# A causal attention and gated MLP kernel: who makes two of the sums of softmax weights, and when the third unit's x is loaded and rounded

## The reference, cut to what matters

```python
Q = _split_heads(x, H)                       # H = 16 heads of 16, B = 8, S = 1024, D = 256
K = _split_heads(x @ Wk + bk, H)
V = _split_heads(x @ Wv + bv, H)             # 1024 wide: 64 per head
scores = jnp.einsum('bhqd,bhkd->bhqk', Q, K) + mask       # causal, not scaled
attn = jax.nn.softmax(scores, axis=-1)
o = jnp.einsum('bhqk,bhkd->bhqd', attn, V)
...
a = x + jax.nn.gelu(o, approximate=False) @ Wf + bf
x = _layernorm(x + a)
...
x = _layernorm(x + (silu(x @ wg.T) * (x @ wu.T)) @ wd.T)   # int weights / 127
```

## Time and profile before

| | |
|---|---|
| time, median of 3 runs | 1847.62 us (1847.26 to 1853.65) |
| the profiled execution's own time | 1849.75 us |
| its span, first to last instruction | 1848.0 us |
| PE busy | 1762.1 us, 95% of the span |
| DVE busy | 1396.5 us, 76% |
| POOL busy | 1221.8 us, 66% (in stage B's slices 0.8 to 0.9, 0.1 to 0.2 in stage C) |
| ACT busy | 1050.4 us, 57% |

### The profile page before, as it was taken

How to read it: one execution, slowest core, us unless ns; L and a number is a source line. 1 busy time by engine, 2 the same in 40 slices (tenths; PEclk the granted TensorE clock), 3 DMA queues, 4 the chain that set the end, 5 groups by cost and what they waited for, 6 DMA issues and landing times. The chain is left out here.

```text
span 1848.0 us, 37611 instructions
## 1 busy us (share of the span) xinstructions
PE 1762.1 (95%) x10304; PEld 961.4 (52%) x10304; DVE 1396.5 (76%) x3417; ACT 1050.4 (57%) x1375; POOL 1221.8 (66%) x1146
## 2 busy tenths in 40 slices
PE   7999999999999999999999999888889999999996
PEld 5444444444444444444444444333466767676763
DVE  4787877778787787777778787886467878787864
ACT  2465665665565565665666565555545555555552
POOL 3488888888888888888888888999512222222221
PEclk9999999999999999999999999999999999999998
DMA  9675657556565655646556565563477565756500
GB/s 323 160 232 160 181 141 203 161 161 188 142 176 170 168 160 159 195 139 185 169 148 196 145 174 143 144 183 99 138 201 175 172 170 172 169 172 170 171 24 23
DMA packets 261152, 303.16 MB, mean 164 GB/s; under 512 B 28240, under 2 KB 177872, under 8 KB 261072
## 3 DMA queue, kind: packets, MB, share of 16 engines
q1 hardware_dynamic: 261072, 302.19, 58.3%
HBM read 174.20 MB, written 127.93 MB: 163 GB/s over the span
## 5 line engine op out<-in xcount | busy, mean ns | idle before, releaser
L802 POOL TENSOR_TENSOR weight_sum<-weight_sum,weights 128x512 f32<-128x512 f32 (+1 forms) x444 | 731.9, 1649 | 151.9 <-DVE weight_sum L1347 115.3
L1161 ACT ACTIVATE weights<-ring 128x1024 f32<-128x1024 f32 x576 | 570.7, 1026 | 221.2 <-PE ring L846 217.8
L846 PE MATMUL o_acc<-weights,v_pair 128*64 128x512 f32 (+3 forms) x3072 | 586.3, 501 | 17.1 <-POOL weights L757 16.4
L837 POOL TENSOR_TENSOR h_lo<-hidden,h_hi 128x512 f16<-128x512 f32 x96 | 114.4, 1193 | 390.2 <-ACT h_hi L1099 390.2
L1312 DVE TENSOR_REDUCE part_max<-ring 128x2 f32<-128x1024 f32 x256 | 301.0, 1217 | 86.4 <-PE ring L846 86.4
L846 PEld LDWEIGHTS o_acc<-weights,v_pair 128*64 128x64 f32 x3072 | 188.3, 136 | 302.7 <-issue 257.0
L1321 DVE CUSTOM_DVE_ANT_0 scrap<-ring,causal,part_max 128x256 bf16<-128x256 f32 (+3 forms) x512 | 251.3, 547 | 70.7 <-PE ring L846 70.4
L1321 DVE CUSTOM_DVE_ANT_0 scrap<-ring,causal 128x128 bf16<-128x128 f32 (+3 forms) x512 | 225.1, 486 | 91.1 <-PE ring L846 90.6
L846 PE MATMUL ring<-q_stack,k_stack 50*128 50x512 f32 (+3 forms) x1536 | 264.3, 382 | 26.1 <-DVE part_max L1312 17.6
L846 PE MATMUL ring<-k_stack,q_stack 48*128 48x512 f32 (+3 forms) x1536 | 256.9, 373 | 0.1
L846 PE MATMUL ring<-wf_sb,g 128*128 128x256 f32 x1024 | 230.5, 380 | 2.6 <-DVE y_pre L1416 1.7
(11 more groups left out here) (125 smaller groups left out, 2070.1 us busy)
## 6 DMA issues: line engine op xcount, KB each, us to landing
v_pairs<-v_unit SPq DMA_DIRECT2D x64, 512.0 KB, 3.5
v_pair<-v_pairs SPq DMA_DIRECT2D x64, 512.0 KB, 5.1
o_heads<-o_pair SPq DMA_DIRECT2D x64, 512.0 KB, 3.2
g<-o_heads SPq DMA_DIRECT2D x16, 2048.0 KB, 8.1
den_wide<-reciprocals SPq DMA_DIRECT2D x32, 1024.0 KB, 13.3
q_stack<-q_rows SPq DMA_DIRECT2D x128, 192.0 KB, 3.7
k_stack<-k_rows SPq DMA_DIRECT2D x128, 192.0 KB, 4.4
q_rows<-x_hi SPq DMA_DIRECT2D x28, 512.0 KB, 3.6
```

What stands on the lines that cost most here:

```text
L802: pool.tensor_tensor(dst, other, weights(t), ALU.add).then_inc(s_add, 1)
L837: pool.tensor_tensor(h_lo[:, f], h32[f % 2][:], h_hi[:, f], ALU.subtract).then_inc(s_hl, 1)
L846: return nc.tensor.matmul(o, l, r, start=start, stop=stop)
L1161: nc.scalar.activation(W[i][:], bank_of("t", i)[:], ACT.Exp).then_inc(s_w, 1)
```

## The change

Four things change. First, `begin_sum` moves from DVE (end of burst 2) to POOL, after the add of group 1. Second, POOL no longer adds group 8 (the ninth group, tile W7); DVE does, as the last sum of all (`last_sum`), at the head of burst 1 of the next step, after it has waited for all of POOL's adds of that pair. A new semaphore `s_add8` tells of it, and PE's `denominators` and ACT's exponential of W7 wait for it. Third, POOL's add of group 11 moves from the next step to the end of its own, and the masks of W7 and W8 now stand side by side. Fourth, the third unit's x: `load_x` comes right after the first stack loads on SP, ahead of five groups of stores, and `x_high` comes in burst 0 of step 0 on ACT.

```diff
-        ADDS = (1, 2, 3, 10, 7, 8, 9, 11)
+        ADDS = (1, 2, 3, 10, 7, 9, 11)
...
             load_stacks(0, 0)
+            load_x(ALONE, True)
             store_early_v(0, 0)
             store_early_k(0, 1)
             store_early_v(0, 1)
             store_early_k(1, 1)
             store_early_v(0, 2)
-            load_x(ALONE, True)
...
+            def begin_sum(rt, n):
+
+                pool.wait_ge(s_w, NU * n + use_of(5) + 1)
+                if rt >= 2:
+
+                    pool.wait_ge(s_den, n - 1)
+                    settle(pool, s_passed["pool"])
+                pool.tensor_tensor(acc1[rt % 2][:], weights(4), weights(5), ALU.add).then_inc(s_add1, 1)
...
                     mask(0, *m)
                     mask(1, *m)
-                if LEAD < r <= PAIRS + LEAD:
-                    add(11, r - LEAD - 1, n - LEAD - 1)
-                if now:
                     mask(2, *m)
                     if r < PAIRS:
-                        for t in (1, 2, 3):
-                            add(t, *m)
+                        add(1, *m)
+                    begin_sum(*m)
                 if r % 4 == 0 and unit_beside(r, it) is not None:
                     x_low(unit_beside(r, it))
                 if now:
+                    if r < PAIRS:
+                        add(2, *m)
+                        add(3, *m)
                     add(10, *m)
                     add(7, *m)
                     mask(7, *m)
-                    add(8, *m)
                     mask(8, *m)
                     add(9, *m)
+                    add(11, *m)
...
                 pe.wait_ge(s_add, NA * (n + 1))
+                pe.wait_ge(s_add8, n + 1)
...
+                    elif i == use_of(8):
+                        act.wait_ge(s_add8, n)
...
-                    if b == 3 and r % 4 == 0 and unit_beside(r, it) is not None:
+                    if b == (3 if r else 0) and r % 4 == 0 and unit_beside(r, it) is not None:
                         x_high(unit_beside(r, it), r == 0)
...
+            def last_sum(rt, n):
+
+                dve.wait_ge(s_add, NA * (n + 1))
+                dst = acc1[rt % 2][:, :, BANK - width_of(8):BANK]
+                v.tensor_tensor(dst, dst, weights(8), ALU.add).then_inc(s_add8, 1)
...
+                    if b == 1 and LEAD < r <= PAIRS + LEAD:
+                        last_sum(r - LEAD - 1, n - LEAD - 1)
...
-                    if b == 2 and LEAD <= r < PAIRS + LEAD:
-                        begin_sum(r - LEAD, n - LEAD)
```

More of the change, by code:

```diff
@@ L292, in build @@
         s_add = sem("sums_made")
+        s_add8 = sem("last_sum_made")
         s_den = sem("den_ready")
@@ L1334, in shift_turn @@
                             shift_parts[:].rearrange("p h m u -> p (h m u)").bitcast(F32)).then_inc(s_shs, 1)
-            def begin_sum(rt, n):
-                dve.wait_ge(s_w, NU * n + use_of(5) + 1)
-                if rt >= 2:
-                    dve.wait_ge(s_den, n - 1)
-                v.tensor_tensor(acc1[rt % 2][:], weights(4), weights(5), ALU.add).then_inc(s_add1, 1)
             def carry_sum(rt, n):
```

## The result

| | before | after |
|---|---|---|
| median of the runs | 1848.62 us (1847.26 to 1853.65, 4 runs) | 1830.3 us (1827.79 to 1832.5, 4 runs) |
| profiled execution, its span | 1848.0 us | 1830.8 us |
| ratio | | 0.9892, 95% interval 0.9876 to 0.9909 |

The changed kernel is 18.3 us faster (1.1%). (The kernel before has four runs here; the median that the forecast started from was that of three, 1847.62.)

The account below looks back on a forecast made before the run. PE was taken to bound the steps with projections, POOL the eight without. Terms -5.0 + 1 + 2 + 1 = -1 us on the median 1847.6 gave 1846.6 us, range 1833 to 1860.

Parts of the forecast that it names:

- Part one: Step 0, third unit's x loaded earlier: PE's 4.34 us wait and slow clock go, -5.0 us, bounds -5.8 and -3.
- The 1.2 us for the clock: Step 0, 42 to 50 us: six matmuls at reduced clock after PE's standstill lose 1.2 us or more, which goes too.
- The second pair's stacks: Step 0: PE wants these stacks 5.5 us earlier while their load time stays; 0.5 us taken off the gain.
- Part two, what goes: Steps with projections: PE's waits at T7 for DVE's maximum of S5 vanish, -1.35 us for four steps.
- Part two, what comes: Four steps with projections: new waits, 1.1 us in k = 0 and 1, 0.25 in k = 3, 0.1 at last_sum.
- The lock: DVE with two SBUF inputs and POOL reading SBUF exclude each other for a whole instruction; two meetings a step, before and after.
- Part three: Eight steps without projections: POOL stays the bound, 0.25 us a step charged for carry_sum queueing, +2 us, bounds -1 and +6.
- Part four: Steps 64 to 66: POOL takes over a sum, but last_sum holds up the first mask; +1 us, bounds -3 and +4.
- A: Rival, the sums are free: new waits covered, PE's 15.6 us come back, 1829 us; chance 0.21.
- Half of A: Half of what rival A expects from the sums coming free: 1837 us.
- B: Rival: DVE waits at last_sum in every step, T3 and T4 slip 0.4 us or more, 1870 us; chance 0.16.
- C: Rival: the early load of x gives nothing, colliding with the stacks or stalling V jobs, 1851.6 us; chance 0.09.

Follow-up runs that it names:

- e1: Kernel before with only the third unit's x loaded and rounded early, sums as they were: 1843.8 us, ratio 0.9964.
- e3: Kernel before without the first sum of the long half (W4 left out of the denominators), a measurement only: 1816.7 us, ratio 0.9828.
- e11: Changed kernel plus a spare addition on DVE of W7 + W7, ahead of the wait of last_sum: 1904.4 us, ratio 1.0302 to the kernel before.
- e7: Changed kernel with the last sum left out (W7 missing in the denominators), a measurement only: 1818.1 us, ratio 0.9828 to the kernel before.
- e12: Changed kernel plus a spare copy of W7 on DVE, ahead of the wait of last_sum: 1860.9 us, ratio 1.0055 to the kernel before.
- e2: Changed kernel with the third unit's x loaded and rounded where it was before, only the sums changed: 1838.4 us, ratio 0.9932 to the kernel before.
- e5: Changed kernel with, in steps k = 0, the next unit's x rounded in burst 1 and split ahead of begin_sum: 1821.2 us, ratio 0.9842 to before.
- e4: Kernel before with begin_sum still on DVE but at the head of burst 4, right ahead of carry_sum: 1854.6 us, ratio 1.0025.
- e6: Kernel e5 with DVE's carry_sum behind the maxima of S6 instead of ahead of them: 1856.1 us, ratio 1.0036 to the kernel before.
- e9: Kernel e5 with begin_sum back on DVE in the steps without projections (56 to 63): 1815.5 us, ratio 0.9815 to the kernel before.

## Why the prediction was wrong, point by point

**Part one, -5.0 us (bounds -5.8 to -3): right.** Measured -6.7 (4.1 to 9.4) by the runs, -3.8 and -5.9 in two traces. x was there at 29.45 us (I had said 29.8) and its split ended at 33.07 (33.3); PE's job came at 37.38 without a wait. The 1.2 us for the clock were not seen in after (the earlier trace rows has 0.79, and so has after) and were in e1. The second pair's stacks cost 0.61 us of named wait in after and 1.89 in e1, where I took 0.5.

**Part two, what goes: the step that failed.** "... the 46 waits make 0.34 us a step: -1.35 us for four steps." The mechanism was right: the waits went. The size was not: they were worth 2.4 to 2.7 us (pitch, e3). I took the named idle time for the price. (15.6 us over 46 waits is 0.34 a wait, not a step; the four waits that follow each other have 1.34 together.) Thirteen times 1.0 to 1.35 us is 13 to 18 us, more than the whole miss of this part, 10.5.

**Part two, what comes: +1.45 said, 1.86 measured.** 0.91 for the split of x and 0.46 at T4 make 1.37 against my 1.1; T8 in k = 3 cost 0.49 against 0.25; k = 1 and 3 cost nothing at `last_sum`. Short waits were again priced by their names.

**The lock: right**, in this kernel and in e11, e3 and e7, and wider than I had put it: e12 shows it for a copy, with one input. That it holds was also why handing a sum to GpSimd frees nothing by itself; the gain is that DVE has no sum ahead of S4 and S5.

**Part three, +2 (bounds -1 to +6): 1.1 lost in the trace,** but hardly for my reason. At full clock POOL is the bound, as I had said, and W4 comes 0.32 us late for it where I had charged 0.25. But less of its list is held up (17.09 us against 17.41 before), and the step is 18.11, 0.1 shorter than before. The loss lies in two steps with a mean granted clock of 0.91, 19.00 and 18.83 us long, in which POOL waits 1.64 and 1.49 us for `carry_sum`; I had no such term. Here is the second of them, and POOL's wait in it:

```profile
1204.71:1223.54 18.83, 17.55 (x104) 7.41 (x104) 14.21 (x40) 10.57 (x13) 16.32 (x17) 0.91 0.61 198
```

```profile
1212.58 3.79 POOL L812 TENSOR_TENSOR weight_sum<-weight_sum,weights 128x512 f32<-128x512 f32 x2 [1.49 <-DVE weight_sum L1352]
```

From 1205 to 1208 us the granted clock is 0.62 and PE is busy throughout; DVE then waits 2.56 us for the scores ahead of `carry_sum`, and POOL for `carry_sum`. The first interval of the stretch is also 1.8 us longer than before and the last 1.2 shorter, both at its borders and not traced further.

**Part four, +1 (bounds -3 to +4): 5 us came back in the trace,** outside these bounds, and without them the kernel would have come out inside the range. From the transpose of step 64 to `g` before takes 31.3 us with a granted clock of 0.89 and 26.02 us of PE's work, after 29.1 with 1.00 and 23.64. POOL waits for `carry_sum` 4.75 and 7.25 us there before, 2.48 and 4.76 after. The other 2.9 us are mostly at PE's wait for `hidden` early in stage C: 5.38 us before, with a granted clock of 0.72 from 1360 to 1372 us, and 2.43 us after, with 1.00 behind it. In e2 and e5, which have the new sums too, the stretch from step 64 to the end gave 2.6 and 2.7 us, in e4, with old sums, 2.3, in e1 -0.3. How much of this is owed to the change stays open.

**The rivals.** A ("every new wait is covered", 0.21) did not come about either: 15.7 us of new named waits stand in the trace. Its test, four steps in 78.4 or less, was missed at 78.94. That the time is near A's 1829 is partly luck: what the change frees was worth almost twice what both had reckoned, new waits took most of it back, and 5 us came from behind step 64. (Half of A is 1836 by its own terms, not 1837.) B was seen only in e6, C nowhere.

## What to carry to other kernels

Price a short wait of TensorE by the distance between the starts around it, with and without the wait, and not by the idle time that the profile names: 0.17 to 0.40 us named cost 0.46 to 0.65 here, while 0.84 named cost 0.91. Where two engines exclude each other, a sum costs both, so in a stretch that one of them bounds ask which engine makes it fastest, and not which has the lower busy share: e9 moved one sum back to DVE there and gained 0.6 us a step, half of what I had expected. And once the first wait goes, look for the next one within its length: here the split of x stood 0.9 us behind, and moving it gave another 9 us.

## What the runs showed of the hardware

A wait that the profile names 0.32 us delays the stream by 0.58. That is the surprise, and a run that takes the cause of the wait away (e3) agrees with the larger number.

An addition of two SBUF tiles on DVE holds up even a tiny POOL instruction until it is done (1.02 us instead of 0.22 for 16 elements a partition). A copy from SBUF to SBUF does so too (0.66 us instead of 0.20) and is itself held up (1.11 us instead of 0.63); a reduction that reads PSUM did not (0.22).

The granted clock after much the same waits of PE was 1.00 in one kernel and 0.79 in another (42 to 50 us in e1 and after), and steps of the same instructions took 18.11 or 18.8 us, with 1.00 and 0.91. Differences of 2 us in such a place can't be laid to an edit from one trace each.
